# Zero rows in place of 64-row matmuls, and VectorE's splitting, scaling and up product handed to GpSimd and ScalarE, in an attention and fp4 feed-forward kernel

## The reference

```python
x = x + xattn(layernorm(x), ctx, Wq, Wk, Wv, Wo, bo)   # 16 heads of 16, float32
x = x + ffn(layernorm(x), w_gate, w_up, w_down)

def xattn(tokens, context, ...):
    Q, K, V = split_heads(tokens @ Wq), split_heads(context @ Wk), split_heads(context @ Wv)
    attn = softmax(Q @ K.T * 0.25)                       # 512 x 1601 for each of 16 heads
    return merge_heads(attn @ V) @ Wo + bo

def fp4_quant_dequant(x):                                # blocks of 16 along the last dim
    scale = maximum(max(abs(block)) / 6, 1e-12)
    return nearest_of([0, .5, 1, 1.5, 2, 3, 4, 6])(abs(block / scale)) * sign * scale

def fp4_linear(x, w): return quant(x) @ quant(w).T
def ffn(x, ...):                                         # inner width 704
    return fp4_linear(silu(fp4_linear(x, w_gate)) * fp4_linear(x, w_up), w_down)
```

## Time and profile before

| | |
|---|---|
| median of 3 runs (lowest, highest) | 3927.74 us (3926.81, 3930.73) |
| span of the profiled execution, its own time from the first to the last instruction | 3925.2 us |
| what lies around that span, against the median | 2.5 us |
| busy: PE, DVE, ACT, POOL | 95%, 76%, 58%, 22% |
| mean granted TensorE clock | 0.983 of 2.4 GHz |
| chain that ended last | PE 78%, DVE 11%, issue 4%, ACT 4% |

### The profile page before, as it was taken

The page is one execution under the profiler, slowest core; times in us unless marked ns, Lnnn a source line. Parts: engine busy times, 40 slices in busy tenths (PEclk is TensorE's granted clock), DMA queues, the critical chain, the costliest instruction groups (busy, mean ns, idle before and its releaser), DMA issues.

```text
span 3925.2 us, 73982 instructions
## 1 busy us (share of the span) xinstructions
PE 3745.4 (95%) x19654; PEld 1618.5 (41%) x19654; DVE 2997.8 (76%) x6641; ACT 2260.4 (58%) x4414; POOL 870.2 (22%) x917
## 2 busy tenths in 40 slices
PE   7999999999999999999999999999999999999997
PEld 2324444344443444434444344443434434344434
DVE  6787787787877877777877777877788777878774
ACT  2656565555655556555565556656565565655562
POOL 2221212222112211222212122221222111222113
PEclk8999999999999999999999999999999999999998
DMA  2222121121211122121121211212111211211100
GB/s 64 50 48 54 22 57 34 33 51 34 50 33 42 39 42 49 26 48 36 39 55 23 53 34 34 53 34 47 36 39 41 43 46 29 45 38 39 37 22 7
DMA packets 148169, 157.83 MB, mean 40 GB/s; under 512 B 58129, under 2 KB 118818, under 8 KB 147746
## 3 DMA queue, kind: packets, MB, share of 16 engines
q1 hardware_dynamic: 147746, 152.78, 17.8%
HBM read 39.53 MB, written 8.39 MB: 12 GB/s over the span
## 4 chain that ended last, share of the span: by engine, by line
PE 78%; DVE 11%; issue 4%; ACT 4%; SPq 1%; DMA 1%; DVEq 0%; POOL 0%; ACTq 0%
PE out_ps L815 17%; PE score_ps L804 16%; PE piece_ps L829 16%; PE work L769 8%; PE work L780 5%; DVE piece_max L1096 4%; PE work L744 3%; ACT probs L913 3%; PE work L737 3%; PE work L743 2%; PE work L735 2%; PE work L722 1%; PE work L759 1%; PE work L753 1%; PE work L727 1%
## 5 line engine op out<-in xcount | busy, mean ns | idle before, releaser
L1096 DVE TENSOR_REDUCE piece_max<-piece_ps 128x1 f32<-128x400 f32 (+1 forms) x4096 | 2144.8, 568 | 680.1 <-PE piece_ps L829 665.2
L913 ACT ACTIVATE probs<-score_ps 128x512 f32<-128x512 f32 (+1 forms) x3328 | 1876.8, 597 | 1085.1 <-PE score_ps L804 1061.0
L829 PE MATMUL piece_ps<-k_stack,q_stack 96*128 96x400 bf16 (+1 forms) x4096 | 1294.0, 339 | 55.5 <-DVE piece_max L1096 51.1
L804 PE MATMUL score_ps<-q_stack,k_stack 99*128 99x512 bf16 (+1 forms) x3328 | 1269.1, 388 | 67.6 <-issue 20.9
L815 PE MATMUL out_ps<-probs,v_ones 128*17 128x512 f32 x6656 | 886.9, 605 | 2.1 <-ACT probs L913 0.9
L804 PEld LDWEIGHTS score_ps<-q_stack,k_stack 99*128 99x128 bf16 (+1 forms) x3328 | 326.1, 99 | 910.1 <-ACT probs L913 639.0
L829 PEld LDWEIGHTS piece_ps<-k_stack,q_stack 96*128 96x128 bf16 x4096 | 389.7, 98 | 700.5 <-DVE piece_max L1096 484.4
L1148 POOL TENSOR_TENSOR h<-h,h_grid 128x704 f32<-128x704 f32 (+1 forms) x68 | 111.2, 1636 | 1106.5 <-DVE h_grid L965 1106.5
L769 PE MATMUL work<-wgu_T,xq_T 128*128 128x256 f32 (+1 forms) x1440 | 345.8, 362 | 0.4 <-ACT xq_T L887 0.4
L769 PEld LDWEIGHTS work<-wgu_T,xq_T 128*128 128x128 f32 x1440 | 258.7, 189 | 49.0 <-ACT xq_T L887 3.4
L815 PEld LDWEIGHTS out_ps<-probs,v_ones 128*17 128x17 f32 x6656 | 110.6, 95 | 277.5 <-issue 233.3
(11 more groups left out here) (142 smaller groups left out, 2846.0 us busy)
## 6 DMA issues: line engine op xcount, KB each, us to landing
k_stack<-k_parts SPq DMA_DIRECT2D x1536, 50.0 KB, 2.2
q_stack<-q_parts SPq DMA_DIRECT2D x1536, 16.0 KB, 1.8
ctx_in<-in_ctx SPq DMA_DIRECT2D x48, 384.0 KB, 3.4
x_in<-in_x SPq DMA_DIRECT2D x16, 512.0 KB, 3.7
resid<-in_x SPq DMA_DIRECT2D x16, 512.0 KB, 3.7
out<-y SPq DMA_DIRECT2D x64, 128.0 KB, 1.9
q_stack<-neg_rows SPq DMA_DIRECT2D x192, 4.0 KB, 1.7
ctx_in<-in_ctx SPq DMA_DIRECT2D x16, 48.8 KB
```

The lines of the kernel that those rows point to most:

```text
L804: pe.matmul(score_ps[0:r, n % SCORE_RING, :], k_stack[:, par, slot(g, j), m * P:m * P + r], q_stack[:, par, slot(g, j), :], start=True, st ...
L829: pe.matmul(piece_ps[:, n % PIECE_RING, 0:hi - lo], q_stack[0:SROWS, par, slot(g, j), t * P:(t + 1) * P], k_stack[0:SROWS, par, slot(g, j) ...
L913: act.activation(probs[0:r, step % 2, j, :], score_ps[0:r, (PER_GROUP * m + j) % SCORE_RING, :], ACT.Exp, scale=SCORE_SCALE).then_inc(prob ...
L1096: dve.tensor_reduce(piece_max[:, row, c:c + 1], piece_ps[:, n % PIECE_RING, 0:piece_at[c + 1] - piece_at[c]], AX_X, ALU.max).then_inc(piec ...
```

## The change

1. No 64-row matmul. The weights of the second chunk are stored with 64 rows of zeros (`Z1`, `ZF`; GpSimd clears them at the start). `k_proj`, `v_proj` and `down` now contract over 128 rows each time. The last chunk of `h_T` transposes the last 128 columns, of which 64 are also in the chunk ahead and meet the zero rows; its two ScalarE copies become one.
2. Splitting. ScalarE only copies the product into `raw` (float32, ring of two, the former `rest`), which frees the `work` bank. GpSimd makes all three parts in four operations (`SPLITS = 4`). ScalarE waits before the copy until GpSimd is through with the same half of `raw`.
3. `max_parts`: VectorE keeps the reduction, the four small operations go to GpSimd.
4. fp4 scaling (`fp4_scale`) of xq, h and the weights: from VectorE to GpSimd.
5. `gate_up`: ScalarE also copies 0.5 x up into `up_half`, ahead of its tanh; VectorE keeps one operation; GpSimd makes the product h.
6. The output rows are written into `x1` in place of `y`. VectorE's five fillings of `k_stack` with ones move from between the start's drains to ahead of the start.

The tables of half steps stay as they are. The diff, cut:

```diff
+SPLITS = 4
+    Z1 = P - C1
+    ZF = P - FTAIL
...
@@ PE
-                    if part == 0:
-                        last = pe.matmul(work[:, 0:w], wk_sb[:, 0, e * P:(e + 1) * P], ctx_T[:, 0, a:a + w], start=True, stop=False)
-                    else:
-                        last = pe.matmul(work[:, 0:w], wk_sb[P - C1:P, 1, e * P:(e + 1) * P], ctx_T[P - C1:P, 1, a:a + w], start=False, stop=True)
+                        pe.wait_ge(padded, 3)
+                    last = pe.matmul(work[:, 0:w], wk_sb[:, part, e * P:(e + 1) * P], ctx_T[:, part, a:a + w],
+                                     start=(part == 0), stop=(part == 1))
...
-                        n = P if c < FT - 1 else FTAIL
-                        last = pe.transpose(work[0:n, (c % 4) * P:(c % 4 + 1) * P], quarter(kind, t).h[:, c * P:c * P + n], ident[:])
+                        a = min(c * P, F - P)
+                        last = pe.transpose(work[:, (c % 4) * P:(c % 4 + 1) * P], quarter(kind, t).h[:, a:a + P], ident[:])
...
@@ ScalarE
-                elif name == "q_proj":
-                    act.copy(q_parts[:, event[1], 0, :], work[:]).then_inc(part0_ready, 1)
...
+                elif name in ("q_proj", "k_proj"):
+                    n = split_number(kind, event)
+                    w = NQ if name == "q_proj" else chunk(event[2])[1]
+                    if not (kind == "start" and n < 2):
+                        act.wait_ge(split_step, count(nxt, SPLITS * 2 * (CHUNKS + 1), SPLITS * (n - 1)))
+                    act.copy(raw[:, n % 2, 0:w], work[:, 0:w]).then_inc(this_drained, 1)
...
-                        act.wait_ge(silu_step, count(old, n * QT, n * t + j))
+                        act.wait_ge(h_ready, count(old, n * QT, n * t + j - 1))
+                    act.mul(up_half[:, (n * t + j) % 2, 0:w], work[:, GW:GW + w], 0.5)
...
@@ VectorE
-                    dve.tensor_copy(neg_parts[:, 0, :], neg_max[:]).then_inc(shift_step, 1)
...
-                    fp4_scale(q.xq, q.xq_small, xq_step, base)
                     fp4_grid(q.xq, q.xq_grid, xq_step, base)
...
-                                             op0=ALU.add, op1=ALU.mult).then_inc(silu_step, 1)
-                    dve.wait_ge(silu_step, count(old, n * QT, n * t + j + 1))
-                    dve.scalar_tensor_tensor(out=q.h[:, j * GW:j * GW + w], in0=tanh_g[:, half, 0:w], scalar=0.5,
-                                             in1=work[:, GW:GW + w], op0=ALU.mult, op1=ALU.mult).then_inc(this_drained, 1)
+                                             op0=ALU.add, op1=ALU.mult).then_inc(this_drained, 1)
...
+            for n in range(PER_GROUP + 1):
+                dve.memset(k_stack[SROWS:SROWS + SHIFT, :, n, :], 1.0).then_inc(cleared, 1)
             body("start", (None, -1))
@@ GpSimd
+            def fp4_scale(src, inverse, ready, total):
+
+                pool.wait_ge(ready, total)
+                pool.tensor_tensor(fp4_blocks(src), fp4_blocks(src), over_block(inverse, src.shape[1] // BLOCK), ALU.mult).then_inc(ready, 1)
...
+                    pool.tensor_tensor(parts[:, half, 0, a:a + w], of, zero[:].broadcast_to([P, w]), ALU.add).then_inc(split_step, 1)
+                    pool.wait_ge(split_step, step(1))
+                    pool.tensor_tensor(of, of, parts[:, half, 0, a:a + w], ALU.subtract).then_inc(split_step, 1)
+                    pool.wait_ge(split_step, step(2))
+                    pool.tensor_tensor(parts[:, half, 1, a:a + w], of, zero[:].broadcast_to([P, w]), ALU.add).then_inc(split_step, 1)
+                    pool.wait_ge(split_step, step(3))
+                    pool.tensor_tensor(parts[:, half, 2, a:a + w], of, parts[:, half, 1, a:a + w],
                                        ALU.subtract).then_inc(split_step, 1)
+                elif name == "max_parts":
...
```

More of the change, by code:

```diff
@@ L404, in build @@
         ctx_T = sb("ctx_T", [P, 2, KW], F32)
-        rest = sb("rest", [P, 2, NQ], F32)
+        raw = sb("raw", [P, 2, NQ], F32)
         stats = sb("stats", [P, QT, 6], F32)
@@ L481, in build @@
         shift_loaded = [sem(f"shift_loaded{i}") for i in range(2)]
-        y_free = [sem(f"y_free{i}") for i in range(2)]
+        x1_free = [sem(f"x1_free{i}") for i in range(2)]
         KSTACKED = 16 * len(STACK)
@@ L742, in fill @@
                     r, a = key_rows(m), m * P
-                    pe.matmul(work[0:r, u * D:(u + 1) * D], ctx_T[:, 0, a:a + r], wv_sb[:, 0, :], start=True, stop=False)
-                    last = pe.matmul(work[0:r, u * D:(u + 1) * D], ctx_T[P - C1:P, 1, a:a + r], wv_sb[P - C1:P, 1, :], start=False, stop=True)
+                    for k in range(2):
+                        last = pe.matmul(work[0:r, u * D:(u + 1) * D], ctx_T[:, k, a:a + r], wv_sb[:, k, :], start=(k == 0), stop=(k == 1))
                 elif name == "maxima":
@@ L1114, in body @@
                         handle(kind, batch, drain)
-                        if kind == "start" and drain[:2] in (("k_proj", 0), ("q_proj", 0)):
-                            write_ones(split_number(kind, drain))
                         drain = None
```

121 lines of the change are left out of this document (59 added, 62 removed).

## The result

The changed kernel takes 3936.13 us (3931.64 to 3941.66, 13 runs) against 3926.81 (3921.45 to 3930.73, 13 runs) for the kernel before: ratio 1.0023, 95% interval 1.0015 to 1.0032. It is slower, by 9 us where 17 were forecast.

A forecast was written before the change was run, and what follows sets the result against it. TensorE's stream, busy 95% of 3925.2 us, was taken as the bound. 3925.2 - 110 - 25 + 58 + 48 + 32 + 5 + 5.5 + 2 + 1 = 3942, 3944 with 2.5 around the span, given as 3945; range 3865 to 3995.

The forecast's parts named there:

- 64-row matmuls: In v_proj, k_proj and down: padding 400 matmuls saves 0.29 us each, 6 us of it worthless at the start; 110 us gained.
- the stop, idle: At half step 38, five GpSimd splits delay ScalarE's copies and an exponential; TensorE idles 3.9 us in 15 batches, 58 us.
- the clock behind it: After each new idle at half step 38, TensorE's clock drops to 1.2 GHz, costing 3.2 us in 15 batches, 48 us.
- maxima's parts: GpSimd's slower chain for the maxima's parts keeps TensorE waiting at L748, 2.1 us a batch: 32 us, bounds 0 and 50.
- relief: Work leaving VectorE ends half of TensorE's 51.1 us of waits for piece reductions: 25 us gained, bounds 0 and 51.
- up product: ScalarE's twelve extra up copies a batch cost 0.3 us a batch: 5 us, bounds 0 and 30.
- start: VectorE's k_stack fillings and longer GpSimd splits make first pieces 7 us later, less 1.5: 5.5 us, bounds 2 and 9.
- first batch: The first batch's weights cost 2 us.
- tail: The end of the kernel costs 1 us.
- GpSimd is late everywhere: Slower rival: GpSimd, busy some 1490 us, delays rstd, xq and h and blocks VectorE's two-port operations; 4000 us, chance 0.20.
- The clock holds: Faster rival: TensorE idles at half step 38 but the granted clock stays 1.00; 48 us off, 3897 us, chance 0.27.
- The stop is hidden: Faster rival: at half step 38 ScalarE clears its backlog before TensorE needs the bank; 58 us less, 3839 us, chance 0.11.

The follow-up runs named there:

- sixteen copies: Kernel before with 64-row matmuls padded by zero rows, plus sixteen unused ScalarE copies at half step 38 in each of 15 batches: 3895.6 us, ratio 0.990.
- maxima as before: Changed kernel with the four small operations for the maxima's parts back on VectorE: 3906.6 us, ratio 0.994 to the kernel before.
- scaling alone: Kernel before with padded zero rows and only fp4 scaling moved to GpSimd (residual output in place): 3802.2 us, ratio 0.966.
- up alone: Kernel before with padded zero rows and only the up product moved to ScalarE and GpSimd, k_stack fillings ahead of the layer norm: 3820.6 us, ratio 0.973.
- zero rows alone: Kernel before with only the padded passes and three clearings on GpSimd, GpSimd and ScalarE otherwise as before: 3814.1 us, ratio 0.970.
- split alone: Changed kernel with maxima's parts, scaling and up product as before, so padded zero rows and GpSimd's split with two raw places: 3919.0 us, ratio 0.997.
- four places: Changed kernel with four places for raw products in place of two, the extra two in x_in: 3883.5 us, ratio 0.988 to the kernel before.
- split as before: Changed kernel with splitting restored: ScalarE casts, VectorE subtracts, GpSimd has two operations: 3831.8 us, ratio 0.975 to the kernel before.
- twelve copies: Kernel before with padded zero rows, plus twelve unused ScalarE copies at half step 38 in each of 15 batches: 3845.7 us, ratio 0.978.
- no zero rows: Changed kernel with 64-row matmuls and transposes as before, all moves to GpSimd and ScalarE kept: 4064.5 us, ratio 1.033 to the kernel before.

## Why the prediction was wrong in size

The direction, the place and the mechanism were right: slower, through the fifth copy at half step 38 and a low clock behind it. The sizes, term by term:

| step | forecast, us | measured, us | from |
|---|---|---|---|
| 64-row matmuls | -110 | -113.5 | spans 3925.2 and 3811.7 |
| the stop, idle | +58 | +53 | 14 x 3.56 + 2.79 |
| the clock behind it | +48 | +24 to +34, directly 32 | sixteen copies; 15 x 5.8 - 53 |
| maxima's parts | +32 | +29.5 | maxima as before |
| relief | -25 | -12 | scaling alone |
| up product | +5 | about 0 | up alone, less its start |
| start | +5.5 | +12.3 | the first exponential |
| first batch | +2 | -4 | -1.8 by the second batch, less a stop of 5.8, plus scaling's 3.5 |
| tail | +1 | +7 | last batch to the end |

These are single comparisons, and they overlap: the maxima's 29.5 us hold 5.2 that also stand in the tail's 7, and the 1.0 us a batch lost at half step 76 has no row. So their sum proves nothing. The stretches of the profiles do not overlap: against the zero rows alone, the changed kernel loses 12.3 us at the start, gains 1.8 in the first batch, loses 104.6 in the next fourteen and 7.0 from there to the end, 122.1 in all, the difference of the spans 3933.8 and 3811.7. Of the 7.4 us a batch, 5.8 are lost by half step 44: 3.56 of idle time and 2.1 of low clock make 5.7.

**The step that failed is "The clock behind it".** It took 3.2 us a batch from the loop turn of the earlier trace rows and carried that price over to each new stop. The two windows beside that of the earlier trace rows:

```profile
1730.00:1735.00 5.00, 1.85 (x9) 0.70 (x6) 0.00 (x0) 1.64 (x4) 0.00 (x0) 0.81 0.20 54
...
1740.00:1745.00 5.00, 5.00 (x24) 1.96 (x24) 2.97 (x8) 2.02 (x4) 0.00 (x0) 0.66 0.56 150
```

With 0.50 between them that is 10.2 us of low clock. This length did not carry over: idle times of 3.56 us, longer than the 3.15 of that turn, were followed by 3.4 or 6.8 us, 5.0 on average, and cost 2.1 us a batch, 32 in all where 48 were forecast. The rate was not too high: 3.2 / 10.2 = 0.31 us for each us of low clock, while the sixteen copies, read directly, give some 0.46 (3.4 us) and 0.41 (6.8 us). Their net figure is lower, 1.57 / 4.5 = 0.35. Some of the price may come back at the loop turns, which is not shown: in the kernel before, five of six turns had 10.2 us of low clock, with sixteen copies three of six, in the changed kernel none, and the others 6.8. "Bounds 0 and 5 a batch" held the truth; the chosen value was the price of a different stop.

That the sum came within 9 us of the time is partly luck: the clock was priced 16 us too high, the relief 13 too high the other way, and start and tail together 13 too low.

**The relief** erred the other way. Of VectorE's four moves only scaling shortens the wait for piece reductions (49.6 to 35.5). It was also misread: of the 51.1 us some 24 came at half steps 4 to 15, half and not most. The unmoved total hides two changes: in the loop the 7.9 us at half steps 92 to 95 are gone, and at 76 to 79 there are 22.5 where 6.1 were. The split's move did nothing for this wait (55.8 us with the split alone) and made a new queue: rstd, the scaled h and the maxima stand behind 4.5 us splits. One case in the changed kernel, at half step 76, POOL and then DVE:

```profile
1675.88 1.16 POOL L1153 TENSOR_TENSOR raw<-raw,q_parts 128x512 f32<-128x512 f32 x1
...
1679.36 0.18 POOL L1179 TENSOR_TENSOR rstd<-mean_var,eps 128x1 f32<-128x1 f32 x1
1679.62 0.55 POOL L1181 TENSOR_TENSOR rstd<-rstd,minus_half 128x1 f32<-128x1 f32 x1
```

```profile
1680.21 1.12 DVE L1025 TENSOR_SCALAR xq<-x,mean_var,rstd 128x256 f32<-128x256 f32 x1 [2.79 <-POOL rstd L1181]
```

TensorE then idles 1.58 us ahead of a piece at 1684.03. That is the rival "GpSimd is late everywhere", true in three places of a batch; the forecast gave it a chance of its own but no share of the sum. Behind the stop it is hidden: with four places the stop's 5.8 us went and 1.7 came at half step 48, since the work behind it was late anyway. So the stop and the queue are one cost of 104 us (split as before), of which a deeper ring alone returns 53.

**The start and the tail.** The start lost 12.3 us to the first score, not 5.5: the forecast had the fillings' 13.6 us but not that the layer norm would then meet GpSimd's splits (3.3 us): the last split of half 0 ended at 42.6 us, not 39.2 (its terms add up to 39.0). Nor did it have the 4.8 us that the zero rows return there. Of the 7.0 us of the tail's row 1.8 are lost in the last batch and 5.2 behind its last exponential. There no exponentials cover GpSimd: scaling and product stand in the chain that TensorE waits for (L771 waits 13.9 us, 6.2 with the zero rows alone). Scaling alone loses 3.5 us in that stretch.

**The zero rows** were sized rightly. By the earlier trace rows the extra is 0.09 + 0.10 + 0.09 = 0.28 us a matmul, not quite the 0.29 of the forecast; the measured 115 us over 400 are 0.29.

**The rivals.** "The clock holds" is refuted for this stop (0.50 behind every one of the 15); with 1.75 us of idle time it would have come true in 14 of 15. "The stop is hidden" is refuted by the 3.56 us. The Trainium skill's "SBUF — State Buffer", Who interferes with whom, says that VectorE's two-port modes and GpSimd exclude each other. The first layer norm's 1.38 and 4.64 us agree with it; the forecast had it inside a rival and not in the start. The longer wait for the maxima (25.5 us with the split alone) does not come from the casts, which took no longer there than in the kernel before. The forecast's reading of the earlier trace rows, that the next cast began only when GpSimd's operation was over, does not hold either. The next cast began inside that operation, which lasts from 1667.13 to 1668.55, and ended just behind it:

```profile
1667.33 1.25 DVE L1015 CAST neg_parts<-neg_rest 128x16 bf16<-128x16 f32 x1
```

The Trainium skill's "TensorEngine Tiling (Array Packing)" was weighed rightly: by the drain of Key Properties the zero rows gain, by "up to twice" they would have lost. The 115 us decide for the gain; no run shows whether a drain is what the 0.29 us are.

Not settled: what chooses between none, 3.4, 6.8 and 10.2 us of low clock.

## What to carry to other kernels

Before work moves to the idle engine, list what its queue already serves in the same stretch and who waits for each: the average load (22% here) says nothing of a burst of five splits. Price a stop by its idle time first, and the clock behind it by the low clock's length times its measured rate, with a range for the length, not by the price of a different stop in the same trace. When one cost hides another, try each remedy by itself: the deeper ring returned half of what the split cost, and the rest was the queue behind it.

## What the runs showed of the hardware

- A float32 matmul with 64 rows, alone between others of 128, cost more than one padded to 128: 115 us for 400 of them, 0.29 us each.
- The idle time alone does not tell the clock. 1.75 us on TensorE left it at 1.00 in 14 of 15 cases (twelve copies), yet 1.4 to 1.5 us were followed by 0.50 in 7 of 14 (no zero rows). Behind 3.49 us it came in 13 of 15, behind 2.27 us (no zero rows) and 3.56 us (changed kernel) in all 14, and it lasted 3.4, 6.8 or 10.2 us. Each us of it cost 0.3 to 0.5 us here.
- GpSimd's float32 subtraction of 512 columns takes 1.16 us, its cast 1.04, one of 704 columns with float32 results 1.39 to 1.68. VectorE's four tensor_scalars of 256 columns take 1.38 us beside an idle GpSimd and 4.64 beside a busy one. A subtraction of 16 columns with a bf16 result took 348 ns on average with the split on GpSimd and 175 before, while the one with a float32 result stayed at 175.
